# A fused transformer layer on one core: which engine issues the first attention's bias loads, and where two small steps of its opening stand

## The reference, cut to what matters

```python
xn = layernorm(x, g_in)
q = (xn @ Wq).reshape(b, n, H, DH).transpose(0, 2, 1, 3) * scale
kv = xn @ Wkv
k, v = (kv[..., :DH], kv[..., DH:])            # one key and one value head for all 16 query heads
k = jnp.concatenate([nk, k], axis=1)           # a "null" key and value, the same for all tokens, goes in front
v = jnp.concatenate([nv, v], axis=1)
sim = jnp.einsum('bhid,bjd->bhij', q, k)
bias = jnp.concatenate([null_col, attn_bias], axis=-1)   # attn_bias: 16 x 512 x 512, shared by the batches
sim = jnp.where(causal_mask, neg, sim + bias)
sim = jnp.where(mask_p[:, None, None, :], sim, neg)
attn = jax.nn.softmax(sim, axis=-1)
out = jnp.einsum('bhij,bjd->bhid', attn, v).transpose(0, 2, 1, 3).reshape(b, n, INNER)
return layernorm(out @ Wo, g_out)
```

## Time and profile before

| | us |
|---|---|
| median of three runs | 2408.55 (2406.16 to 2410.59) |
| span of the profiled execution, first to last instruction | 2401.5 |
| median of the runs less that span (launch and end, which the trace does not cover) | 7.05 |
| first score matmul of pair 0 starts (TensorE, line 558) | 63.64 |
| TensorE busy | 2053.0, 85% of the span |
| mean granted TensorE clock, as a share of full | 0.955 |

### The profile page before, as it was taken

How to read it: one execution, slowest core, us unless ns; L and a number is a source line. 1 busy time by engine, 2 the same in 40 slices (tenths; PEclk the granted TensorE clock), 3 DMA queues, 4 the chain that set the end, 5 groups by cost and what they waited for, 6 DMA issues and landing times.

```text
span 2401.5 us, 33727 instructions
## 1 busy us (share of the span) xinstructions
PE 2053.0 (85%) x11536; PEld 1111.7 (46%) x11536; DVE 1528.3 (64%) x3276; ACT 1161.6 (48%) x2718; POOL 1068.8 (45%) x840
## 2 busy tenths in 40 slices
PE   2999899999989998985678976889999998873997
PEld 1555555555555555552345863223333332221664
DVE  1345868686776768685964545667667766434776
ACT  0776666666666666662112341345555454541221
POOL 0104747474756658474576532112222201117686
PEclk9999999999999999997889997899999999996998
DMA  7315352434410000005035643111111150203232
GB/s 250 116 36 170 101 194 88 132 108 139 136 34 13 14 7 5 14 5 152 25 112 166 194 155 90 43 35 40 45 53 50 40 193 18 73 10 106 78 92 75
DMA packets 175729, 204.60 MB, mean 85 GB/s; under 512 B 19305, under 2 KB 157417, under 8 KB 175306
## 3 DMA queue, kind: packets, MB, share of 16 engines
q1 hardware_dynamic: 116826, 112.57, 14.8%
q0 software_dynamic: 16752, 45.84, 6.3%
q10 hardware_dynamic: 41984, 44.04, 5.4%
HBM read 83.75 MB, written 114.46 MB: 83 GB/s over the span
## 4 chain that ended last, share of the span: by engine, by line
PE 59%; DVE 14%; POOL 9%; ACT 9%; issue 5%; DMA 2%; ACTq 2%; SPq 1%; POOLq 0%; DVEq 0%
PE ps L1863 11%; POOL prod L829 8%; ACT m_pt L2022 6%; PE ps L561 4%; PE ps L588 4%; PE ps L547 3%; PE ps L572 3%; PE ps L598 3%; DVE sc L841 3%; PE ps L1877 3%; DVE pb L712 3%; PE ps L2224 3%; PE ps L1285 3%; PE ps L2232 2%; PE ps L1821 2%
## 5 line engine op out<-in xcount | busy, mean ns | idle before, releaser
L1954 DVE TENSOR_REDUCE m_mx<-ps 128x2 f32<-128x1024 f32 x256 | 311.6, 1224 | 172.3 <-PE ps L1842 171.6
L712 DVE CUSTOM_DVE_ANT_0 pb<-ps,bias,snl 128x128 f32<-128x128 f32 (+3 forms) x512 | 260.4, 547 | 226.6 <-PE ps L561 223.7
L2022 ACT ACTIVATE m_pt<-ps 128x1024 f32<-128x1024 f32 x256 | 260.5, 1024 | 289.2 <-PE ps L1863 289.2
L829 POOL TENSOR_TENSOR prod<-qs,kvs 128x1024 f32<-128x1024 f32 x120 | 283.7, 2390 | 171.8 <-issue 133.0
L829 POOL TENSOR_TENSOR prod<-sc,kvs 128x1024 f32<-128x1024 f32 x120 | 280.5, 2369 | 101.9 <-ACT sc L947 85.8
L1863 PE MATMUL ps<-m_q,m_k 32*128 32x512 f32 x1024 | 274.2, 647 | 50.8 <-ACT m_pt L2022 39.9
L907 ACT ACTIVATE pb<-pb,mst 128x129 f32<-128x129 f32 (+3 forms) x512 | 283.4, 560 | 16.9 <-DVE mst L712 14.9
L1842 PE MATMUL ps<-m_k,m_q 32*128 32x512 f32 x1024 | 276.3, 660 | 8.9 <-DVE m_mx L1954 8.3
L561 PE MATMUL ps<-kz,qT 64*128 64x128 f32 (+3 forms) x1024 | 185.5, 441 | 0.0
L2041 POOL DMA_INDIRECT m_yg<-ye_scratch,e_pos x64 | 63.1, 986 | 270.4 <-DVE m_x L1942 233.1
L572 PE MATMUL ps<-ident,pb 128*128 128x128 f32 x1280 | 179.8, 279 | 0.5 <-DVE mst L712 0.4
(11 more groups left out here) (329 smaller groups left out, 3837.4 us busy)
## 6 DMA issues: line engine op xcount, KB each, us to landing
xh_scratch<-zt SPq DMA_DIRECT2D x43, 768.0 KB, 8.2
xe_scratch<-zt ACTq DMA_DIRECT2D x32, 1024.0 KB, 4.5
ye_scratch<-e_ys SPq DMA_DIRECT2D x36, 256.0 KB, 2.1
hw_w<-in_w SPq DMA_DIRECT2D x16, 512.0 KB, 6.0
xin<-in_x SPq DMA_DIRECT2D x8, 512.0 KB, 3.6
bias<-in_fside ACTq DMA_DIRECT2D x8, 512.0 KB, 10.6
y_scratch<-e_y SPq DMA_DIRECT2D x8, 512.0 KB, 3.2
m_x<-y_scratch SPq DMA_DIRECT2D x8, 512.0 KB, 4.1
```

The costliest lines, as they stand in the source:

```text
L712: dv.tensor_tensor_reduce(pb.ap[:, j, SEG[t]:SEG[t] + n], rS.of(("S", b, p, t, j)).ap[:, 0:n], k.bias[:, h, CAUSAL[t]:CAUSAL[t + 1]], -1.0 ...
L829: e.tensor_tensor(out, one, two, ALU.mult).then_inc(*k.c.did(*product_done(step, b, t, u)))
L1954: dv.tensor_reduce(x.ap[:, t, 64 * half:64 * half + 64].rearrange("p (i r) -> p i r", i=2)[:, :, 16], score_ring(k, b).of((b, g, t, half)) ...
L2022: ac.activation(p.ap[:, 2 * half:2 * half + 2, :], k.qE.of((b, g, kt, half)).ap, ACT.Exp).then_inc(*did("m_exp", b, g, kt, half))
```

## The change

1. ScalarE issues only bias group 0 (4 transfers) at its head; then it waits for the constant `mhalf` and runs one `Exp` over a 128x4 tile into a new tile `early_exp`, which nothing reads. The other 7 groups are issued by SyncE.
2. SyncE's first loads are reordered (`nk` comes ahead of `wk`, `wq` goes behind `wv`), and everything from `wo` and `nv` on goes to a new function `sync_rest`, run at a new step `rest` behind `queries` of pair 0. SyncE's `keys` step now issues the batch's mask row first, and then waits for `turn_x` and issues the next `xin`.
3. `fold_value` leaves the opening and stands at the head of turn m = 4 (`FOLD_AT`).

```diff
+FOLD_AT = 4
...
     out = [("ln_x", 0), ("norm_x", 0), ("fold_key",), ("turn_x", 0, 0), ("turn_x", 0, 1), ("keys", 0), ("vals", 0),
-           ("fold_value",), ("queries", 0, 0)]
+           ("queries", 0, 0), ("rest",)]
...
+        if m == FOLD_AT:
+            out.append(("fold_value",))
...
+    k.early_exp = top("early_exp", [P, NT])
...
     once("gin", cols(k.gin), ins["g_in"])
-    once("wq", cols(k.wq), ins["cond_wq"].rearrange("(c p) n -> p c n", p=P))
+    once("nk", cols(k.nk), ins["cond"][0:1, :].broadcast_to([P, DH]))
     for j in range(2):
         sp.dma_start(k.wk[:, :, j, :], wkv[:, :, 0:DH]).then_inc(*did("d_wk", j))
     once("wv", cols(k.wv), wkv[:, :, DH:2 * DH])
-    once("nk", cols(k.nk), ins["cond"][0:1, :].broadcast_to([P, DH]))
+    once("wq", cols(k.wq), ins["cond_wq"].rearrange("(c p) n -> p c n", p=P))
     once("nb", cols(k.nb), ins["null_bias"].rearrange("(o n h) -> o n h", o=1, n=1).broadcast_to([P, NT, H]))
+    sync_one_steps(k, sp, w, k.order1)
+
+
+def sync_rest(k, sp):
...
+    load_bias(k, sp, 1)
+    once("wo", cols(k.wo), ins["cond_wo"].rearrange("(c p) n -> p c n", p=P))
+    load_bias(k, sp, 2)
     for j in range(2):
         sp.dma_start(k.nv[DH * j:DH * j + DH, :], nvc).then_inc(*did("d_nv", j))
-    once("wo", cols(k.wo), ins["cond_wo"].rearrange("(c p) n -> p c n", p=P))
+    for g in range(3, 8):
+        load_bias(k, sp, g)
     once("gout", cols(k.gout), ins["g_out"])
...
     once("bout", cols(k.bout), row(ins["attn_bout"]))
-    sync_one_steps(k, sp, w, k.order1)
...
         if step == "keys":
             b = key[0]
+            m8 = k.mrow.of(b)
+            w.wait_ge(m8.room)
+            sp.dma_start(m8.ap[:, :], ins["mask"][b:b + 1, :].bitcast(U8).broadcast_to([P, S])).then_inc(*did(f"d_mrow{b % 2}", b))
             if b + 1 < NB:
                 w.wait_ge(at("turn_x", b, 0), at("turn_x", b, 1))
                 sp.dma_start(cols(k.xin), xv[b + 1]).then_inc(*did("d_xin", b + 1))
-            m8 = k.mrow.of(b)
-            w.wait_ge(m8.room)
-            sp.dma_start(m8.ap[:, :], ins["mask"][b:b + 1, :].bitcast(U8).broadcast_to([P, S])).then_inc(*did(f"d_mrow{b % 2}", b))
+        elif step == "rest":
+            sync_rest(k, sp)
...
-def scalar_bias(k, ac):
+def load_bias(k, e, g):
+
     fv = k.ins["fside"].rearrange("h (t p) k -> t p h k", p=P)
-    for g in range(8):
-        for t in range(NT):
-            ac.dma_start(k.bias[:, 2 * g:2 * g + 2, CAUSAL[t]:CAUSAL[t + 1]],
-                         fv[t][:, 2 * g:2 * g + 2, 0:P * (t + 1)]).then_inc(*k.c.did(f"d_bias{g}", t))
+    for t in range(NT):
+        e.dma_start(k.bias[:, 2 * g:2 * g + 2, CAUSAL[t]:CAUSAL[t + 1]],
+                    fv[t][:, 2 * g:2 * g + 2, 0:P * (t + 1)]).then_inc(*k.c.did(f"d_bias{g}", t))
...
-        scalar_bias(k, ac)
+        load_bias(k, ac, 0)
+        w.wait_ge(at("mhalf", 0))
+        ac.activation(k.early_exp[:, :], k.mhalf[:, :], ACT.Exp).then_inc(*k.c.did("early_exp", 0))
         scalar_one(k, ac, w, k.order1)
```

More of the change, by code:

```diff
@@ L439, in sync_one @@
     wkv = ins["cond_wkv"].rearrange("(c p) n -> p c n", p=P)
-    nvc = ins["cond"][1:2, :].rearrange("a d -> d a")
     def once(name, dst, src):
@@ L451, in sync_one, with once @@
     once("wv", cols(k.wv), wkv[:, :, DH:2 * DH])
-    once("nk", cols(k.nk), ins["cond"][0:1, :].broadcast_to([P, DH]))
+    once("wq", cols(k.wq), ins["cond_wq"].rearrange("(c p) n -> p c n", p=P))
     once("nb", cols(k.nb), ins["null_bias"].rearrange("(o n h) -> o n h", o=1, n=1).broadcast_to([P, NT, H]))
+    sync_one_steps(k, sp, w, k.order1)
+def sync_rest(k, sp):
+    ins, did = k.ins, k.c.did
+    nvc = ins["cond"][1:2, :].rearrange("a d -> d a")
+    def once(name, dst, src):
+        sp.dma_start(dst, src).then_inc(*did("d_" + name, 0))
+    load_bias(k, sp, 1)
+    once("wo", cols(k.wo), ins["cond_wo"].rearrange("(c p) n -> p c n", p=P))
+    load_bias(k, sp, 2)
     for j in range(2):
         sp.dma_start(k.nv[DH * j:DH * j + DH, :], nvc).then_inc(*did("d_nv", j))
-    once("wo", cols(k.wo), ins["cond_wo"].rearrange("(c p) n -> p c n", p=P))
+    for g in range(3, 8):
+        load_bias(k, sp, g)
     once("gout", cols(k.gout), ins["g_out"])
```

## The result

The changed kernel takes 2381.88 us (median of 4 runs, 2374.61 to 2387.34) against 2407.36 before (4 runs). The ratio is 0.9908, 95% interval 0.9887 to 0.9928: 22 us faster by the ratio, 25.5 by the medians, where 29.9 was forecast (2378.6). A second set of the same two kernels gave 0.9898 (0.9879 to 0.9917). The profiled execution has a span of 2372.8 us, 28.7 less than before, and its own time is 2374.61, the fastest of the four runs.

What follows compares the result with a forecast made beforehand. TensorE bounds the whole kernel, ScalarE's bias issue queue the first 38 us. Opening gain 38.1 less 8.2 for the fold gives 29.9 us: 2408.55 to 2378.6, range 2371 to 2387 (8 in 10).

Steps and rivals of the forecast that it cites:

- ScalarE's queue: Opening: with 4 issues left, ScalarE is free at about 5 us; normalizing starts at 10.7 instead of 39.70, 29.0 us earlier.
- The early table load: ScalarE's opening: loading early hides the table load in the wait for the statistics, worth 1.3 of the 29 us.
- The key fold: Opening, VectorE: wq lands at 12.4, fold ends at 17.7, half a microsecond ahead of need; upper price 2.3 us.
- Values and queries: TensorE's opening: old distances kept, queries directly after values, first score at 24.5; 1 us allowed for slow clock, gain 38.1.
- The fold at turn 4: Head of turn 4: stall 3.2 us plus matmuls 3.5 to 6.6, each clock case given half; cost taken as 8.2.
- rival C: Turn 4: fold runs at lower clock, full 9.8 us and up to 3 of slow scores; gain 25, time 2383; chance 0.11.
- SyncE's list: SyncE's 40 rest transfers land by 48 us; group 1 and batch 1's mask row each keep 8 us cover; cost nothing.
- Rivals A and B: SyncE's rest list. A: late, price 8 us, time 2387, chance 0.08. B: so late the kernel is slower, 0.03.
- Contention: Scores of pairs 0 to 2 run while loads run; TensorE loses nothing.
- The shift lasts: From turn 5 to the end, every step comes 30 us earlier; what the first score gains, the end gains.
- The offset of 7.05 us: Runs' median lies 7.05 us above the profiled span of 2401.5; the difference is carried over to the forecast time.

Runs made afterwards that it cites:

- warm: Changed kernel plus small unread matmuls keeping TensorE busy in the opening (120 before the first transpose, more between transposes): 2375.77 us, ratio 0.9888.
- fold_split: Changed kernel with the value fold cut in two, VectorE's clear and copies at turn 3, TensorE's matmuls at turn 4: 2374.73 us, ratio 0.9874.
- no_table: Changed kernel without the early Exp: 2382.77 us, ratio 0.9918.
- half_on_act: Changed kernel with bias groups 0 to 3 (16 transfers) issued by ScalarE at its head instead of group 0 alone: 2380.34 us, ratio 0.9912.
- quick: Changed kernel with wq issued right behind gin, and ScalarE issuing bias group 0 only after its table load and xin's landing: 2370.63 us, ratio 0.9859.
- quick_split: Changed kernel with reordered first transfers (wq early, bias group 0 after xin) and the value fold in two, no busy matmuls: 2365.25 us, ratio 0.9846.
- fold_only: Kernel before the change with only the value fold moved to the head of turn 4 of batch 0: 2405.57 us, ratio 0.9994.
- after_again: Changed kernel run again, nothing edited: 2378.19 us, ratio 0.9898 to the kernel before.
- fold_open: Changed kernel with the value fold back in the opening between vals and queries, nv and wo issued behind nb: 2377.07 us, ratio 0.9889.
- quick_warm_split: Changed kernel with reordered first transfers, busy TensorE matmuls in the opening (100 before the first transpose) and the value fold in two: 2364.93 us, ratio 0.9829.
- hold: Changed kernel with reordered transfers, busy matmuls, split fold, and 10 small matmuls behind each of batch 0's first three value groups: 2364.01 us (one run).

## Why the prediction was right, and where it was off

**ScalarE's queue: right.** Normalizing at 10.61 against 10.7. The dose of four groups confirms that it is the issues that hold ScalarE. The part of SyncE's new order in this (`nk` ahead, the rest behind the queries) was not run by itself.

**The early table load: wrong in a term.** I gave it 1.3 of the 29 us, "without it the load would stand in the chain". It does not: the load is an instruction of its own that waits for nothing, and runs as soon as ScalarE's stream comes to it. The 1.28 us in the kernel before stood behind the queue, and go with the queue. The sum to 10.7 did not rest on it. The Trainium skill (ScalarE: Activation LUTs, What ACT_TABLE_LOAD costs) would have put 2.7 us with its drain in the place of 1.3. The trace agrees with its 1.28 for the load and shows no drain: in the kernel before normalizing starts 0.01 us behind the load.

**The key fold: right in its time, wrong in its safety.** `wq` was there at 12.66 (12.4 forecast), the fold done at 17.94 (17.7). That was the earliest of six profiles with these first transfers, which have 12.66 to 14.43; the slow keys hid it. My bounds for it had an upper price of 2.3 us; in `warm` it came to 3.6 with the clock on top, as soon as the keys were quick.

**Values and queries: the term that was mis-sized.** "I take 1 us for this" for a slow clock. The same code from normalizing to the first score took 18.5 and 18.9 us in the two profiles of the changed kernel, 15.8 in `fold_split` and 13.6 in `no_table`, where the old distances, fold aside, give 23.94 - 10.13 = 13.8. So the old distance is the lucky end, and the mean cost of the clock is 2.9, not 1 (3.0 with the 15.8, 18.9 and 15.8 of `half_on_act`, `quick` and `quick_split`). With the scatter of `xin` (normalizing starts at 10.5 to 12.5 us in six profiles with the changed kernel's first transfers: 10.45, 10.61, 11.64, 12.37, 12.44, 12.50, on the mean 1.0 later than I had it), that is 1.9 + 1.0 = 2.9 of the 4.4 us between the forecast gain and that of the medians. The rest, 1.5, is less than the interval of the ratio leaves open (some 5 us either way). In the profile the shortfall lies in this term alone: the first score gained 34.5 of 38.1, the fold cost 8.5 for 8.2.

**The fold at turn 4: right.** Stall 3.07 (3.2), matmuls 5.30 (3.5 to 6.6, by the clock), sum 8.5 (8.2). The clock fell, as rival C had it, but no slow scores followed. My cause for it, "behind the stall", is not what the rows show: in the changed kernel it fell 0.3 us ahead of the stall, at the end of the value matmuls. Over all profiles it is open how much is the stall's doing. In the seven with this stall (3.07 to 3.18 us) the clock fell every time, four times 0.1 to 0.3 us ahead of it and three times 0.2 to 1.5 us into it (at 101.20 in `fold_only`, 74.13 in `no_table`, 81.55 in `half_on_act`); in the six without a stall there it fell in two. So I gave each case half, and with the stall it was the lower clock seven times out of seven. What the kernel before lost to the fold in the opening, 10.1, and what it costs now, 8.5, differ by as much as the clock makes of either. The rule of the Trainium skill that I weighed (TensorE: Matmul & The Clock Gate, HAM oscillation: a wait between groups of matmuls lets the clock drop) holds in `warm`, where the clock fell at 19.22 us, 3.0 us into the wait of 3.61. In turn 4 it gave the right clock, but in four of the seven profiles that clock was down before the wait began. The page's own example has waits of some 3 to 5 us, so it spoke less firmly for a drop behind 3.2 us than I put it.

**SyncE's list: right, with the cover larger than thought.** The 40 issues of `rest` ended at 45.1, `mrow` of batch 1 went out then and was used at 64.77: 16 us of slack (with its 3.7 to land). Rivals A and B had no ground: SyncE's 28 bias issues took 0.83 us each on the mean (2.04 + 6.30 + 14.98), not 1.18. Group 1 was later than forecast, filled at 25.5 instead of 23, wanted at 35.8; VectorE waited for no later group.

**Contention: right.** Keys of 1.98 us in `warm` and value matmuls of full speed in `no_table` run beside a DMA share of 0.88 and 0.97.

**The shift lasts: right.** 26.0 at turn 4, 29.5 at 1108 us, 28.7 at the end, and nothing gave it back. From the first score of turn 4 to the end it is 2288.9 us before, 2286.2 in the changed kernel and 2281.1 to 2293.1 in all profiles. That the profile's 28.7 comes so near the 29.9 of the forecast is luck: the 26.0 are the change's, the rest is the low clock after 224 us in the kernel before.

**The offset of 7.05 us** that I carried is not launch and end: the changed kernel's execution has 1.8 between span and time. The other 5 us were the distance of one quick execution to the median.

## What to carry to other kernels

Here 32 DMA issues of 10.5 MB held the engine that made them for 37.65 us, 16 of them for 16.55 and 4 for 2.03. So look for a bulk load in the stream of an engine with early work; leave there only what the first step needs, and put the rest on an engine whose next job is late. After that the opening was set by the first transfer's landing, so hold back what goes out beside it (normalizing from 10.5 to 12.5 down to 8.5 us here). Moving a step that all engines wait in from one place to another was worth nothing that these runs can tell; splitting it so that its slow half runs beside other work takes the stall out (3.1 us in the profile, too little for the times alone).

## What the runs showed of the hardware

- In an opening, TensorE at 1.2 GHz is no matter of the first few microseconds. Counted from the first transpose, in the ten profiles without busy matmuls, it stayed there 6.4 to 8.1 us in six (6.4 in the kernel before and in `no_table`), 16.5 in the changed kernel (busy without a pause from 14.8 us on) and 22.4 to 22.6 in three (`after_again`, `fold_open`, `quick`). The steps are the same up to the values. What decides between them is not shown.
- Where the clock is up, it can fall within or behind a run of small matmuls (64 and 16 columns) that keeps TensorE's row at full busy: at 69.50 us in `quick_warm_split`, and in four of the six openings named under `hold`. The scatter of the time from run to run, 10 us and more, is of the size of what such stretches cost; that it is their sum was not shown.
- One transfer of 512 KB was used 5.7 to 7.8 us after its issue beside the other queue's 1.3 MB (6.88 to 8.94, issued at 1.17, in six profiles), and 3.7 to 4.0 us after it with nothing from that queue (4.90, 4.91, 5.07 and 5.13 in four profiles). So it scattered by 2 us with the other queue and by 0.2 without.
- The two issues of `nv`, 64 elements of 4 bytes each, held SyncE 4.26 us in the kernel before and 1.40 in the changed one. What makes the difference is not shown.
